# A fused block of attention and FFN: gelus of two steps summed by one GpSimd call, W2 five steps behind W1, another order in the turn

## The reference

```python
h = tok_ref(x, ...)                      # patches of (64, 3, 224, 224), projected to 128, class token, times positions
h = concat([h, txt], axis=1)             # (64, 193, 128)
h = h + attn_ref(layernorm(h), ...)      # qkv, group norm, 8 heads of 16 (q, k of 8), relative positions, softmax, group norm
h = h + ffn_ref(layernorm(h), ...)
# ffn_ref
top_p, _ = top_k(softmax(x @ Wg), 2);  top_p = top_p / sum(top_p)
for i in range(2):
    w_in = x * top_p[..., i:i+1]
    g = gelu(einsum('btd,edf->ebtf', w_in, W1) + b1, approximate=False)      # all 8 experts, dff 512
    out = out + einsum('ebtf,efd->btd', g, W2) + sum(b2)
```

## Time and profile before

| | |
|---|---|
| median of three runs | 3173.65 us |
| profiled execution | 3172.15 us, its span 3170.3 |
| busy in the span: TensorE, VectorE, ScalarE, GpSimd | 96%, 62%, 59%, 46% |
| mean granted TensorE clock | 0.99 of full; 1.00 in the turns |
| one turn | 90.25 us, 30 of them nearly alike |
| TensorE, one W1 step (L426 to the end of L430's issue) | 0.53 us |
| TensorE, one W2 part (two L417) | 0.65 us |
| TensorE, transposes of the output (L440) and of v (L470) | 0.43 and 0.5 us |
| a_rep, from its DMA's issue to landing | 9.7 us |
| u_scratch, the DMAs before it, from issue to landing | 2.2 us each |

### The profile page before, as it was taken

How to read it: one execution, slowest core, us unless ns; L and a number is a source line. 1 busy time by engine, 2 the same in 40 slices (tenths; PEclk the granted TensorE clock), 3 DMA queues, 4 the chain that set the end, 5 groups by cost and what they waited for, 6 DMA issues and landing times.

```text
span 3170.3 us, 61793 instructions
## 1 busy us (share of the span) xinstructions
PE 3053.5 (96%) x19776; PEld 2514.4 (79%) x19776; DVE 1951.6 (62%) x4141; ACT 1873.4 (59%) x4370; POOL 1462.0 (46%) x1350
## 2 busy tenths in 40 slices
PE   6986999999999999999999999999999999999998
PEld 5876888777788888777888887778888877788886
DVE  5634566666666666666666666666666666666665
ACT  4642556665555566655565666555655665555557
POOL 1001445555444445554444455544444555544446
PEclk9998999999999999999999999999999999999999
DMA  9971011111110011111100111111101111111010
GB/s 208 224 200 38 18 26 28 28 27 27 26 28 14 20 28 28 28 26 26 28 20 13 28 28 28 26 28 26 27 6 28 28 28 26 28 26 28 4 26 6
DMA packets 92173, 121.58 MB, mean 38 GB/s; under 512 B 8414, under 2 KB 86558, under 8 KB 87710
## 3 DMA queue, kind: packets, MB, share of 16 engines
q1 hardware_dynamic: 87714, 118.24, 15.9%
q10 hardware_dynamic: 4432, 2.99, 0.4%
HBM read 106.23 MB, written 14.97 MB: 38 GB/s over the span
## 4 chain that ended last, share of the span: by engine, by line
PE 73%; DVE 8%; issue 6%; ACT 5%; DMA 0%; POOL 0%; DVEq 0%; ACTq 0%; POOLq 0%; SPq 0%
PE bank L417 14%; PE bank L517 6%; PE bank L426 6%; PE bank L518 6%; PE bank L562 6%; PE bank L563 6%; PE bank L530 6%; PE bank L430 4%; PE bank L427 4%; PE bank L544 3%; PE bank L462 3%; DVE dl L769 3%; DVE gelu L603 2%; ACT gelu L822 2%; PE bank L572 2%
## 5 line engine op out<-in xcount | busy, mean ns | idle before, releaser
L896 POOL TENSOR_TENSOR gelu<-gelu 128x386 f32<-128x386 f32 x1024 | 1077.1, 1073 | 309.6 <-ACT gelu L823 303.2
L822 ACT ACTIVATE gelu<-bank,b_s 128x386 f32<-128x386 f32 x1024 | 593.9, 580 | 644.4 <-DVE gelu L603 628.5
L417 PE MATMUL bank<-gelu,w_s 128*128 128x386 f32 x2048 | 821.0, 487 | 0.3 <-POOL gelu L896 0.3
L603 DVE TENSOR_TENSOR gelu<-bank,ratio 128x386 f32<-128x386 f32 x1024 | 563.6, 557 | 311.6 <-PE bank L430 308.5
L823 ACT ACTIVATE gelu<-gelu,b_s 128x386 f32<-128x386 f32 x1024 | 625.1, 610 | 0.0
L426 PE MATMUL bank<-x_hi,w_hi 128*128 128x386 f32 x1024 | 544.6, 532 | 19.6 <-ACT gelu L822 8.2
L864 ACT ACTIVATE lp<-bank,mx 128x193 f32<-128x193 f32 x800 | 328.6, 425 | 173.8 <-DVE mx L709 173.4
L517 PE MATMUL bank<-k_f,q_bd 128*128 128x193 f32 x1600 | 402.4, 333 | 15.2 <-DVE a_bd L699 8.7
L518 PE MATMUL bank<-rw,a_bd 128*128 128x193 f32 x1600 | 393.4, 328 | 0.0
L417 PEld LDWEIGHTS bank<-gelu,w_s 128*128 128x128 f32 x2048 | 373.1, 189 | 18.5 <-POOL gelu L896 1.2
L909 POOL TENSOR_TENSOR gst<-gst,half 128x4 f32<-128x4 f32 x32 | 32.6, 1018 | 721.0 <-DVE gst L691 721.0
(11 more groups left out here) (131 smaller groups left out, 4575.4 us busy)
## 6 DMA issues: line engine op xcount, KB each, us to landing
a_rep<-u_scratch SPq DMA_DIRECT2D x32, 1600.0 KB, 9.7
xt<-in_x SPq DMA_DIRECT2D x192, 196.0 KB
txt_s<-in_txt SPq DMA_DIRECT2D x32, 128.0 KB, 2.1
u_scratch<-k_f SPq DMA_DIRECT2D x32, 100.0 KB, 2.2
u_scratch<-q_f SPq DMA_DIRECT2D x32, 100.0 KB, 2.2
out<-o_s SPq DMA_DIRECT2D x64, 48.5 KB
out<-o_s SPq DMA_DIRECT2D x64, 48.0 KB
rv<-in_rel_v SPq DMA_DIRECT2D x1, 2624.0 KB, 14.0
```

The source lines that it names most:

```text
L417: mm(yb[:, 0:T2], w2_s[:, f, :], gelu1[:, f % RING, :], start=(f == 0), stop=(f == NF - 1)).then_inc(S["w2_done"], 1)
L603: v.tensor_tensor(gelu2[:, f % RING, :], zb[f % 2][:, 0:T2], ratio[:, :], ALU.mult).then_inc(S["z2_done"], 1)
L822: a(gelu1[:, f % RING, :], zb[f % 2][:, 0:T2], ACT.Gelu, bias=b1_s[:, f:f + 1]).then_inc(S["g_done"], 1)
L896: g.tensor_tensor(gelu1[:, f % RING, :], gelu1[:, f % RING, :], gelu2[:, f % RING, :], ALU.add).then_inc(S["hs_done"], 1)
```

## The change

Four things change. GpSimd sums the gelus of an even step and the odd one after it in one call over 2 x 386 columns (L898 of the new file), issued with every odd step; `hs_done` now counts pairs, and VectorE and TensorE wait for pairs. `LAG` is 5, so there are five `w2t`. The add of 1.0 in `gate2` and the add of the bias in `hres` are tensor_tensor instructions with a broadcast operand instead of tensor_scalar (a third column of `half` holds the 1.0). And the list has another order.

```diff
-LAG = 4
+LAG = 5
 SCHEDULE = (
-    "c qs0 c qs1 vt am0 qs2 c log0 am1 am2 log1 log2 qs3 hkeep log3 log4 log5 am3 log6 log7 log8 txt log9 mean1 log10 log11 qs4 var1 log12 c tr0 c bc1 c tr1 inv rel0 tr2 rel1 tr3 rel2 tr4 rel3 tr5 rel4 tr6 rel5 rel6 proj pv0 gmean rec0 pv1 gvar rec1 place0 c place1 c omean gaff c ovar c c c c c nqk c c oaff c c onorm c oh2 c c mean2 c c var2 c top c c gate c gate2 c c bcast w2t w2t xin w2t nv a a w2t ot a otr ocopy hres"
+    "c c vt qs0 am0 qs1 qs2 qs3 c hkeep c log0 am1 am2 txt log1 qs4 log2 log3 mean1 log4 log5 log6 am3 log7 log8 log9 log10 log11 var1 log12 c tr0 bc1 c c inv tr1 rel0 tr2 rel1 tr3 rel2 tr4 rel3 tr5 c rel4 tr6 rel5 rel6 c proj pv0 gmean pv1 rec0 rec1 place0 gvar place1 c c omean c c gaff ovar c c c c oaff c c c onorm c oh2 c nqk nv mean2 c c var2 top c gate c c c gate2 c w2t bcast w2t xin w2t w2t a w2t ot a otr hres a ocopy"
...
-                pe.wait_ge(S["hs_done"], n * NF + f + 1 + RING)
+                pe.wait_ge(S["hs_done"], n * (NF // 2) + f // 2 + 1 + RING // 2)
...
-                ring_wait(dve, S["hs_done"], f, n)
+                dve.wait_ge(S["hs_done"], n * (NF // 2) + f // 2 + 1)
...
-                    v.tensor_scalar(dl[0:GW, 4:8], ep[0:GW, 0:4], 1.0, None, ALU.add).then_inc(S["e1_ready"], 1)
+                    v.tensor_tensor(dl[0:GW, 4:8], ep[0:GW, 0:4], half[0:GW, 2:3].broadcast_to([GW, 4]), ALU.add).then_inc(S["e1_ready"], 1)
...
-                    v.tensor_scalar(hres[:, :], h2[:, :], b2x2[:, :], None, ALU.add).then_inc(S["hres_done"], 1)
+                    v.tensor_tensor(hres[:, :], h2[:, :], b2x2[:, :].broadcast_to([P, T2]), ALU.add).then_inc(S["hres_done"], 1)
...
-            def gelu_sum(f, n):
-                pool.wait_ge(S["g_done"], n * (2 * NF) + 2 * f + 2)
-                g.tensor_tensor(gelu1[:, f % RING, :], gelu1[:, f % RING, :], gelu2[:, f % RING, :], ALU.add).then_inc(S["hs_done"], 1)
+            def gelu_sums(f, n):
+                pool.wait_ge(S["g_done"], n * (2 * NF) + 2 * f + 4)
+                s = slice(f % RING, f % RING + 2)
+                g.tensor_tensor(gelu1[:, s, :], gelu1[:, s, :], gelu2[:, s, :], ALU.add).then_inc(S["hs_done"], 1)
...
-                if f >= SUM_LAG:
-                    gelu_sum(f - SUM_LAG, n)
+                if f > SUM_LAG and (f - SUM_LAG) % 2:
+                    gelu_sums(f - SUM_LAG - 1, n)
...
-                if s == "w2t" and f >= NF - SUM_LAG:
-                    gelu_sum(f, n)
+                if s == "w2t" and f >= NF - SUM_LAG and f % 2:
+                    gelu_sums(f - 1, n)
```

More of the change, by code:

```diff
@@ L263, in fused_block @@
         b2x2 = sb("b2x2", [P, 1])
-        half = sb("half", [P, 2])
+        half = sb("half", [P, 3])
         w1_hi = sb("w1_hi", [P, NF * P], F32R)
@@ L792, in _ @@
             v.memset(half[:, 0:1], -0.5).then_inc(z, 1)
+            v.memset(half[:, 2:3], 1.0)
             v.memset(half[:, 1:2], 2.718281828459045).then_inc(z, 1)
@@ L802, in _ @@
             dve.sem_inc(S["os_ready"], 2)
-            dve.sem_inc(S["hs_done"], RING)
+            dve.sem_inc(S["hs_done"], RING // 2)
             dve.sem_inc(S["w2_done"], RING)
```

## The result

The changed kernel takes 3305.35 us (median of four, 3302.62 to 3305.78) against 3174.23 of the kernel before on the same chip: a ratio of 1.041, with an interval of 1.0392 to 1.0428. The forecast had the sign, and at 3242 us about half of the size: 68 us more instead of 131. The profiled execution has a span of 3303.6 us.

A forecast was written before the change was run, and what follows sets the result against it. TensorE bounds the kernel, busy 88.88 of 90.25 us a turn, so only its waits count. 0.7 + 2.1 - 0.5 = +2.3 us a turn over thirty turns gives +69, 3242 us; range 3138 to 3286, the forecast's own 3215 to 3270.

The forecast's parts named there:

- Term 2: In the logits: mean1 waits for h while VectorE's products alternate with GpSimd's calls; +2.1 us a turn, bounds 0 and 3.0.
- Term 1: Start of the turn: steps done ahead, without W2 parts beside them, wait for gelus; +0.7 us a turn.
- Term 3: Rest of the turn: 1.7 us of waits to win, 1.2 put back for new holds; -0.5 us a turn.
- top stands directly behind var2, before GpSimd's sum starts: its hold is gone: At L762 near the turn's end: the hold goes, worth 0.35 us a turn, but L766 meets the pair sum.
- TensorE's cover hides L773's hold: At the gate: a pair sum can hold L773 for 1.5 us, against some 2.4 us of TensorE's cover.
- The pair sum: GpSimd's sum of two steps: taken as 1.55 us from the 640-column row; other estimates 1.44, 1.80 and 1.98.
- A: In the logits: L665 isn't held, TensorE waits 1.3 us; +1.0 us a turn, 3204 us; chance 0.15.
- B: GpSimd's queue before the maxima is shorter, mean1 waits 0.7 at most, four waits go: -0.8 a turn, 3149 us; chance 0.30.
- C: It cancels: logits hold about half as forecast, turn's end wins 1.7 us; within 7 us of before; chance 0.07.
- all four waits of term 3: TensorE's waits at nqk (0.31 us), onorm (0.39), top (0.35) and before the broadcast L462 (0.64), 1.7 us a turn together.
- D: Pair sums hold L766, the add and L773 in full, pair takes 1.98: +4.0 us a turn, 3294 us; chance 0.08.
- The form of the add: At L769: as tensor_tensor it waits only for GpSimd's operation in flight, not its whole queue; no size of its own.

## Why the prediction was right or wrong

- **Term 2, the logits: right in its mechanism, its number in part by luck.** 2.7 us of waiting where 2.6 were worked out, by the chain named: a_bd, a_bd and L665 alternating with GpSimd. Undoing the place of txt alone gave back what was expected, 75 us. But the chain held two pair sums of 1.55 us that took 1.84. The time came back elsewhere: TensorE and the first sum were a little earlier than counted, and a held operation ends sooner behind the one that it waits for than its own length (L665 0.15 us behind the fifth q_bd, at 1384.29 against 1384.14, where 0.34 was counted).
- **Term 1, the turn's start: right in kind, over-sized.** 7.81 - 6.86 - 0.53 = 0.42 us instead of 0.7. To the fourth step behind the first it is 4.68 (1368.68 to 1373.36), where 4.76 was counted. From there to the logits it is 3.13 instead of 3.34, in which nothing waits: the busy parts were rounded up.
- **Term 3, the rest of the turn: wrong, sign included.** It was put at -0.5 us; 3.15 - 0.42 - 2.7 + 0.5 = +0.5 us came. The step that failed is "top stands directly behind var2, before GpSimd's sum starts: its hold is gone". L762 does start before the sum (1449.88 against 1449.98), but while GpSimd's power still runs, and the sum that follows at once goes first. It is held 1.96 us, and the step beside it costs TensorE 1.36 us more than a free one (2.54 against 1.18), where the hold before cost 0.35 and nothing was forecast. A second step failed in part: that TensorE's cover hides L773's hold. L773 was held 1.47 us as worked out; 0.2 us of it shows before the broadcast, and with the late W2 parts behind it 0.73 us were lost there, where the 0.64 before the broadcast were to be won. As said came the end of nqk's wait and a wait of mean2 (0.39 us, forecast 0.1 to 0.5). That the add was free, 0.15 us, was luck: it started 0.01 us ahead of a pair sum.
- **The pair sum: 1.84 us, not 1.55.** The prediction had bounds of 1.44 and 1.98 and chose the 640-column row; the row chosen was of another operation, a product with broadcast operands. The estimate of 1.80 from the Trainium skill (GPSIMD Engine Reference, "Elementwise — side-by-side cycle accounting") agrees with the rows of L898.
- **A term is missing: the clock, put at nothing.** A wait of TensorE was priced at its own length. This one brings the granted clock to half in two turns of three, 1.66 us each, 33 us in all; the filled wait took 35 us off. At 3270 us, with the wait filled, the kernel stands inside the stated range; so the clock is what puts 3305 above it. The profile before had falls of the clock outside the turns, in the stretches of the first pairs, and the prediction did not use them.
- **Rivals.** A fell with L665's 1.37 us. B needed a chain shorter than TensorE's way to mean1, and it was 2.7 us longer. C needed half of term 2 and all four waits of term 3; neither came. D's number, 3294, is the nearest to 3305, but not by its reasons: L773 was held as it said, L766 and the add were free, the pair sum did not take 1.98 us, and without the clock the turn grew by 3.15 us and not by 4.0. "The form of the add" as a gain, used in B and in the part on VectorE and GpSimd, fell with the run that changed the two instructions alone.

In sum, forecast and measured, us a turn: start +0.7 and +0.4; logits +2.1 and +2.2; rest -0.5 and +0.5; clock 0 and +1.1; together +2.3 and +4.3 (rounded each by itself). The kernel with short sums shows the common cause of the logits, of what top and the broadcast lose and of the clock's fall: the length of GpSimd's sums, most of it by what they hold on VectorE. The start of the turn and the wait of mean2 belong to the order.

What stays open: which of two waiting instructions goes first where GpSimd has several operations in a row. The a_bd products got in after one operation; the add of four columns had to wait for two or three (issued 0.05 to 0.5 us into the first of them), and L762 for one or two. The runs show no rule that fits all of these. It also stays open what decides on the clock's fall. In the turns the waits of up to 1.1 us in the run with txt back had none behind them; a wait of 1.5 us had one in 18 of 29 turns, one of 2.55 us in 20, and one of 1.4 us in 16 of 29 with txt early but in 2 of 29 with txt back. So the length of the single wait doesn't decide it alone.

## What to carry to other kernels

Count an engine's operation by what it keeps another engine from doing, not by the engine's own load: GpSimd was half idle, and the length of one of its calls decided 196 us. When instructions with two SBUF operands stand in a chain that the bound engine waits for, keep long GpSimd calls away from that place or the chain away from them, and re-check every place when the length or the order changes, since holds move. Price a wait of TensorE of 1.4 us and more at more than itself, here up to 1.66 us more, and look for the granted clock behind it.

## What the runs showed of the hardware

- A GpSimd sum over 128x386 takes 1.02 us and over 128x772 1.84 us: pairing saves 0.19 us a pair, a tenth; over 128x8 it takes 0.2.
- A VectorE instruction of four columns takes 0.15 us free and up to 3.58 us held (L769 in the old order with pair sums, 3.27 in the median); tensor_scalar and tensor_tensor are held alike (2665 and 2657 ns in the median at the same place).
- With sums of 0.2 us the same VectorE instructions are free (L762 0.165 us, L773 0.162), and the kernel is 196 us faster.
- TensorE's clock fell to half for 3.4 us, beginning 0.2 to 1.4 us after the end of a wait of 2.55 us, in 20 turns of 29; 1.9 us of useless matmuls in that wait made the kernel 35 us faster. In other runs it fell behind waits of 1.4 and 1.5 us too, in 16 and 18 turns of 29.
